# Attention products of four heads in every second eighth, over eight probability tiles

## The reference

```python
h = tok(x)                                   # a recurrence over 8 steps, 32 x 250 tokens of 64 features
h = h + attn(layernorm(h))
h = h + ffn(layernorm(h))                    # top 2 of 16 experts, then a layernorm

def attn(x):                                 # B=32, S=250, E=64, 8 heads
    xn = ln(x)
    Q, K, V = xn @ W_q, xn @ W_k, xn @ W_v   # per head
    sqdist = max(q2 + k2 - 2 * Q @ K.T, 0)
    scores = exp(-gamma * sqdist)            # no softmax
    out = scores @ V                         # per head, then @ W_o
```

## Time and profile before

| | us |
|---|---|
| median of 3 runs | 893.88 (892.8 to 894.4) |
| the profiled execution | 894.32 |
| its span, first to last instruction | 892.0 |
| PE busy | 812.0 (91%) |
| DVE busy | 771.9 (87%) |
| ACT busy | 595.7 (67%) |
| POOL busy | 457.1 (51%) |
| mean granted TensorE clock | 0.989 of full speed |

### The profile page before, as it was taken

The page is one execution under the profiler, slowest core; times in us unless marked ns, Lnnn a source line. Parts: engine busy times, 40 slices in busy tenths (PEclk is TensorE's granted clock), DMA queues, the critical chain, the costliest instruction groups (busy, mean ns, idle before and its releaser), DMA issues.

```text
span 892.0 us, 17432 instructions
## 1 busy us (share of the span) xinstructions
PE 812.0 (91%) x4384; PEld 446.9 (50%) x4384; DVE 771.9 (87%) x1970; ACT 595.7 (67%) x1089; POOL 457.1 (51%) x600
## 2 busy tenths in 40 slices
PE   1699879999999999999999999899999999999994
PEld 1244445656555655556555555444444444444441
DVE  5376668999999999999999998899999999999984
ACT  0365577877888777788778874666666666666652
POOL 7270254434445444445344441257777666777645
PEclk9999979999999999999999999999999999999997
DMA  4400022111221111221112210000000000000000
GB/s 113 132 15 2 2 47 48 25 36 37 48 47 41 29 29 43 47 47 24 37 33 47 48 39 10 0 1 8 12 6 6 6 6 6 6 6 6 7 11 12
DMA packets 22741, 25.16 MB, mean 28 GB/s; under 512 B 12752, under 2 KB 21648, under 8 KB 22576
## 3 DMA queue, kind: packets, MB, share of 16 engines
q1 hardware_dynamic: 22384, 23.93, 11.4%
q10 hardware_dynamic: 320, 0.79, 0.4%
HBM read 5.37 MB, written 2.43 MB: 9 GB/s over the span
## 4 chain that ended last, share of the span: by engine, by line
PE 54%; DVE 28%; issue 9%; ACT 3%; DMA 2%; SPq 1%; POOL 1%; DVEq 0%; ACTq 0%; POOLq 0%
DVE prob L773 9%; PE bank L1063 8%; PE bank L1176 8%; PE bank L1194 8%; PE bank L1111 7%; DVE m L789 6%; PE bank L991 5%; PE bank L1087 5%; PE bank L1089 4%; DVE gated L258 4%; DVE lg L866 2%; DMA xw<-xparts 2%; PE bank L981 1%; DVE qk L783 1%; DVE lg L870 1%
## 5 line engine op out<-in xcount | busy, mean ns | idle before, releaser
L773 DVE TENSOR_SCALAR prob<-prob,cap_hi,cap_lo 125x250 f32<-125x250 f32 x512 | 230.6, 499 | 27.3 <-ACT prob L542 23.5
L607 ACT ACTIVATE relu<-bank,b_sb 128x500 f32<-128x500 f32 x256 | 160.8, 674 | 99.9 <-PE bank L1194 79.6
L420 POOL TENSOR_TENSOR sq<-sq 125x256 f32<-125x256 f32 x128 | 97.1, 765 | 174.7 <-ACT sq L556 107.6
L542 ACT ACTIVATE prob<-bank 125x500 f32<-125x500 f32 x256 | 147.7, 586 | 52.2 <-PE bank L1089 49.2
L258 DVE TENSOR_TENSOR gated<-relu,wb 128x500 f32<-128x500 f32 x224 | 159.0, 724 | 6.3 <-ACT relu L607 4.1
L1063 PE MATMUL bank<-prob,u 125*64 125x250 f32 x1024 | 136.5, 387 | 20.9 <-DVE prob L773 20.2
L1176 PE MATMUL bank<-gated,w_sb 128*64 128x500 f32 x512 | 135.3, 607 | 12.2 <-DVE gated L258 12.2
L1087 PE MATMUL bank<-m,s 128*125 128x500 f32 x256 | 112.6, 440 | 0.0
L1194 PE MATMUL bank<-s,w_hi 128*128 128x500 f32 x256 | 110.1, 430 | 0.0
L1063 PEld LDWEIGHTS bank<-prob,u 125*64 125x64 f32 x1024 | 62.5, 136 | 87.6 <-DVE prob L773 45.0
L1089 PE MATMUL bank<-m,s 112*125 112x500 f32 x256 | 101.3, 396 | 0.0
(11 more groups left out here) (176 smaller groups left out, 1476.4 us busy)
## 6 DMA issues: line engine op xcount, KB each, us to landing
m<-m SPq DMA_DIRECT2D x128, 125.0 KB, 2.3
out<-res SPq DMA_DIRECT2D x16, 125.0 KB
xa<-xparts SPq DMA_DIRECT2D x4, 281.2 KB
w1raw<-in_w SPq DMA_DIRECT2D x1, 1024.0 KB
xw<-xparts SPq DMA_DIRECT2D x4, 140.6 KB
w_sb<-in_w SPq DMA_DIRECT2D x1, 512.0 KB
m<-s SPq DMA_DIRECT2D x32, 15.6 KB
xparts<-x_part SPq DMA_DIRECT2D x1, 375.0 KB, 4.0
```

Of the source, the lines that this page charges most:

```text
L542: act.activation(prob[n % 4][:, :, :], bank[5 + n % 3][0:T, 0:C].rearrange("p (h l) -> p h l", h=2), ACT.Exp).then_inc(b_exp, 1)
L607: act.activation(relu_sb[g % 4][:, :], bank[4 + g % 4][:, 0:C], ACT.Relu, bias=b1_sb[:, g:g + 1]).then_inc(c_relu, 1)
L773: last = dve.tensor_scalar(part, part, cap_hi[0:T, h:h + 1], cap_lo[0:T, h:h + 1], ALU.min, ALU.max)
```

## The change

The number of probability tiles becomes `PROBS = 8`. TensorE makes no products in odd eighths; in an even eighth `v` it makes the two groups `v - 2` and `v - 1`, one behind the other (in eighth 0 those numbered 6 and 7 of the pair before). ScalarE's wait before an exponential asks for the products of four eighths before in place of two.

```diff
--- before.py
+++ after.py
@@ -163,7 +163,7 @@
         m1, s2, u_sb, sq, sq2, prob, y_att = phase(
             ("m1_", 2, [128, H, C], F32R), ("s2_", 2, [S_ROWS, C], F32R), ("u", 2, [T, CH, H * D], F32), ("sq", 2, [T, H, D], F32),
             ("sq2_", 2, [T, H, D // 2], F32),
-            ("prob", 4, [T, 2, L], F32), ("y_att", 2, [128, L], F32))
+            ("prob", PROBS, [T, 2, L], F32), ("y_att", 2, [128, L], F32))
         relu_sb, gated, (y_moe,), (yt,), (yt2,), (stats2,), (aggr2,), (inv2,), (yz,), (res,), wb = phase(
             ("relu", 4, [128, C], F32), ("gated", 8, [128, C], F32), ("y_moe", 1, [128, C], F32),
             ("yt", 1, [T, CH, D], F32), ("yt2_", 1, [T, CH, D], F32), ("stats2_", 1, [T, CH, 6], F32), ("aggr2_", 1, [T, CH, 2], F32),
@@ -538,8 +538,8 @@
                 def exps(v, c):
                     n = 2 * v + c
                     act.wait_ge(b_sc, 16 * (p - 1) + n + 1)
-                    wait(act, b_pv, 8 * (p - 1) + v - 1)
-                    act.activation(prob[n % 4][:, :, :], bank[5 + n % 3][0:T, 0:C].rearrange("p (h l) -> p h l", h=2),
+                    wait(act, b_pv, 8 * (p - 1) + v - 3)
+                    act.activation(prob[n % PROBS][:, :, :], bank[5 + n % 3][0:T, 0:C].rearrange("p (h l) -> p h l", h=2),
                                    ACT.Exp).then_inc(b_exp, 1)
 
                 def unit(k):
@@ -769,7 +769,7 @@
                     dve.wait_ge(b_exp, 16 * (p - 1) + n + 1)
                     for hh in range(2):
                         h = (2 * v + hh) % H
-                        part = prob[n % 4][:, hh, :]
+                        part = prob[n % PROBS][:, hh, :]
                         last = dve.tensor_scalar(part, part, cap_hi[0:T, h:h + 1], cap_lo[0:T, h:h + 1],
                                                  ALU.min, ALU.max)
                     last.then_inc(b_cap, 1)
@@ -1061,7 +1061,7 @@
                 h = (2 * v + hh) % H
                 for c in range(2):
                     last = pe.matmul(bank[1][64 * c:64 * c + 64, 0:L], u_sb[jj][:, 2 * b + c, h * D:(h + 1) * D],
-                                     prob[(2 * v + c) % 4][:, hh, :], start=h == 0, stop=h == H - 1)
+                                     prob[(2 * v + c) % PROBS][:, hh, :], start=h == 0, stop=h == H - 1)
                 if hh == 1:
                     last.then_inc(b_pv, 1)
 
@@ -1129,11 +1129,12 @@
                             unit(rest.pop(0))
                     for k in rest:
                         unit(k)
-                    for hh in range(2):
-                        if v == 0 and old2:
-                            products(p - 2, 7, j, hh)
-                        if v > 0 and old:
-                            products(p - 1, v - 1, o, hh)
+                    for n in (v - 2, v - 1) if v % 2 == 0 else ():
+                        for hh in range(2):
+                            if v == 0 and old2:
+                                products(p - 2, n + 8, j, hh)
+                            if v > 0 and old:
+                                products(p - 1, n, o, hh)
                     if old2 and v == 1:
                         if new:
                             pe.wait_ge(b_s1, p + 1)
@@ -1157,8 +1158,9 @@
 
             def step_b_tail(p, j, old2, old, new, ln):
                 if isinstance(p, int) and p == PAIRS + 1:
-                    products(p - 2, 7, j, 0)
-                    products(p - 2, 7, j, 1)
+                    for n in (6, 7):
+                        for hh in range(2):
+                            products(p - 2, n, j, hh)
                 else:
                     step_b(p, j, old2, old, new, ln)
 
@@ -1253,6 +1255,7 @@
 PREP_GA = PREP_GX + 6 * LANES
 PREP_G = PREP_GA + 26
 GATE_D = 9
+PROBS = 8
 POOL_GROUPS = (6, 8)
 LOGITS = -1
 GATE = 18
```

## The result

The changed kernel takes 883.59 us (median of 4 runs, 883.49 to 883.99) against 894.11 before: a ratio of 0.9874 with a 95% interval of 0.9853 to 0.9894, 1.3% faster. The forecast was 904.5, slower. The profiled execution took 883.49 us with a span of 881.3; before it was 892.0.

What follows compares the result with a forecast made beforehand. The prediction took a loop of TensorE (9.2 us) and VectorE (18 us) as the bound. 14 x 0.62 + 2.1 - 0.2 = + 10.6 us on 894.3 gave 904.9, less 0.4 for the median: 904.5; range 890 to 911.

Steps and rivals of the forecast that it cites:

- What happens between group 7 and the scores of eighth 3: TensorE's stretch in each step: four groups instead of three, so the scores of eighth 3 come 0.62 us later.
- TensorE's part: The loop from group 7 to eighth 3's exponential, 9.2 us; TensorE time there is paid in full.
- VectorE's part: The loop's other 18 us, up to the caps of eighth 7; changed stalls between VectorE and POOL priced at nothing.
- one stall of 0.95 us either way: Bound on VectorE's caps meeting POOL's work: one such stall more or less per step, 0.95 us.
- a rival of 0.08: One stall of VectorE's caps fewer in each of 14 steps: - 2.7 us, 891; chance 0.08.
- The end: Last attention step, without projections: groups 6 and 7 stand in the chain and end 2.1 us late.
- the structure of the loop: Each 27.20 us step: TensorE holds 9.2 us from group 7 to exponential 3, VectorE the other 18 us.
- the 0.99 us before group 6: TensorE's wait there goes, but becomes waiting in front of groups 6 and 7, at least 1.4 us.
- the two faster ones: TensorE is the bound, 878, or its 0.99 us wait before group 6 is not replaced, 880; chance 0.14 together.
- a step of 27.8: Sign of a right forecast: 27.8 us from one step to the next in place of 27.20.
- 0.8 us of idle time before eighth 1: Sign of a right forecast: VectorE idles some 0.8 us before the first caps of eighth 1.
- a step under 27.2: Sign of a wrong forecast: a period from step to step under 27.2 us.

Runs made afterwards that it cites:

- the first experiment: The changed kernel with one wait more, TensorE waiting for the caps of eighth 7 before group 6: 896.92 us, 1.0019 to before.
- The short additions: POOL's additions of the halves of squares made over 8 instead of 256 columns from the second pair on: kernel before 889.04 us, changed kernel 872.98 us.
- groups 0 and 1: The kernel before with eight tiles and only groups 0 and 1 merged, in eighth 2: 886.99 us, 0.992.
- groups 2 to 5: The kernel before with eight tiles and only groups 2 and 3 merged in eighth 4, 4 and 5 in eighth 6: 892.74 us, 0.9977.
- the swap: The changed kernel with VectorE in eighth 6 making both pairs of caps, then the two subtractions: 882.28 us, 0.9846.
- groups 6 and 7: The kernel before with eight tiles and only groups 6 and 7 merged, in eighth 0: 895.29 us, 1.0011.
- still less in TensorE's part: The changed kernel with groups 0, 1 and 2 at the end of eighth 3, group 3 in 4, groups 4 and 5 in 6: 885.1 us, 0.9897.
- the tiles: The kernel before with eight probability tiles and ScalarE's looser wait, every group where it was: 894.69 us, 0.9992.
- the changed kernel again: The changed kernel unaltered, run once more on the same chip as its neighbours: 883.34 us, 0.9862.

## Why the prediction was wrong

**The step that failed** is in "What happens between group 7 and the scores of eighth 3": "Eighth 0: + 0.86 (group 6 ahead of group 7; both wait for the caps of eighth 7, since TensorE runs in order)". In-order execution holds group 7 back behind group 6, not group 6 behind group 7's wait. Group 6 needs only the caps of eighth 6, and the text had itself found 1.4 us of idle TensorE right there. It counted them as waiting time in front of both groups and did not put group 6 into them. The term was 0; with the assumed wait put into the code it was 0.86 (27.22 less 26.36). Over 14 steps that is 12.0 us, more than the whole forecast change of 10.6.

**TensorE's part otherwise** was right in its place and too small in its size: - 1.10 + 0.86 = - 0.24 was forecast, - 0.40 measured. 0.10 of this is the output's transposes. They take 0.35 us (342.99 to 343.34) behind an ordinary matmul and took 0.45 (323.51 to 323.96) behind products; I had looked only at the way in. A second group behind the first costs about 0.84 instead of 0.86.

**VectorE's part** was priced at nothing "since both chains shift together", and was - 0.40 us a step. They don't shift together in eighths 1 to 3: there POOL's additions wait for VectorE's reductions (line 783), but the caps wait for exponentials, and so for TensorE. The stall of eighth 3's caps, which counted, became one of eighth 2's, where it takes idle time. The bound that the text gave, one stall of 0.95 us either way, held this; it belonged in the forecast and not in a rival of 0.08. A second piece is that eighth 4's exponential ended just as VectorE came to it, 0.04 us before its caps. The text did not look at that tie.

These three make up the difference: 0.62 forecast against - 0.81 measured is 1.43, and 0.86 + 0.16 + 0.40 = 1.42.

**The end** was to cost 2.1 us. From the last step's group 7 to the next one it took 19.50 us before and 19.12 after: it gave 0.4. Here too groups 6 and 7 were counted behind the caps. With the assumed wait the same distance, measured on group 7, is 19.97.

**Right were** the structure of the loop, that the 0.99 us before group 6 are replaced by a wait for xn, that TensorE's savings as such are not the gain (by its own estimate the mergings of groups 2 to 7 save 0.8 us a step; they gave 0.18), and that the tiles are worth nothing. Of the rivals, the two faster ones named 878 and 880 with TensorE as the bound. The sign was theirs; the mechanism was not, as the first experiment shows. The signs named for a right forecast answer clearly: a step of 27.8 and 0.8 us of idle time before eighth 1 are absent, and the latter is present as soon as the wait is added; a step under 27.2, which it named as a sign of being wrong, is there.

The Trainium skill, TensorEngine Tiling (Array Packing), Key Properties, says that changing the tiling mode drains TensorE. The 0.10 us at each boundary fit this, though no run here separates the mode from whatever else changes there; and merging groups away from TensorE's part of the loop gave little all the same. The Trainium skill, SBUF — State Buffer, Who interferes with whom, says that VectorE in a two-port mode and POOL block each other for a whole instruction. The short additions agree: with them the stretched caps of eighths 1 to 4 vanish.

## What to carry to other kernels

When work is moved up to a wait on an in-order engine, ask for each piece which wait is its own, and fill it into the idle time in front of the later wait before anything is added to the loop. A stall that two engines cause each other has a place as well as a length: moving the work by half a microsecond can shift it from the loop into idle time or back, so its bound belongs to the forecast itself. Where two waits end within 0.1 us of each other, neither can be priced alone.

## What the runs showed of the hardware

TensorE's clock, in two executions of the changed kernel, in the same place of the expert phase. From windows of the first one (length, busy us and counts by engine, then the granted clock):

```profile
555.00:558.00 3.00, 0.30 (x3) 0.23 (x4) 2.90 (x7) 0.69 (x2) 1.96 (x2) 1.00 0.00 0
558.00:562.00 4.00, 4.00 (x12) 1.46 (x8) 3.70 (x14) 1.86 (x4) 0.00 (x0) 0.57 0.00 0
```

and of the second:

```profile
556.50:559.30 2.80, 0.25 (x2) 0.23 (x4) 2.73 (x6) 0.50 (x2) 1.73 (x2) 1.00 0.00 0
559.30:563.30 4.00, 4.00 (x18) 1.64 (x16) 3.83 (x14) 2.14 (x5) 0.00 (x0) 1.00 0.00 0
```

In both TensorE idles 2.70 us. Behind it the granted clock has a mean of 0.57 over 4 us in the first, so it was at the lower level of 1.2 GHz for most of them, and it stayed at 2.4 GHz in the second. At the lower level a matmul of 500 columns starts 0.42 us after the one before it instead of 0.23, and the round is 1.6 us longer. The same instructions with the same idle time have both outcomes, so such a dip in one profile must not be read as a cost of the change. The other profiles of this case say the same. Of the twelve in which TensorE idles 2.7 us there, six have a first round of 21.85 to 22.04 us with the clock down (the changed kernel, the added wait, groups 0 and 1, groups 2 to 5, the short additions in the changed kernel, the swap) and six have 20.45 to 20.47 without it (before, groups 6 and 7, the short additions in the kernel before, still less in TensorE's part, the tiles, the changed kernel again). The steps lie before it and are free of it.

A cap of VectorE alone takes 0.41 us; one that meets an addition of POOL takes up to 0.97, and one that meets xn 1.38 in most steps. Summed over the 512 caps, what they take beyond 0.41 us each is some 48 us, in the kernel before and after alike; what differs is where it lies.
